# Output product of self-attention: one of eight stationary tiles dropped, its rows carried by transfers between buffers

## What is computed

```python
Wdkv = x @ latent_w + latent_b
q = jnp.einsum('btc,hcl->bhtl', x, Wd_w) + Wd_b[None, :, None, :]
scores = jnp.einsum('bhtl,bsl->bhts', q, Wdkv) / sqrt(d_head)     # causal mask
attn = jax.nn.softmax(scores, axis=-1)
y = jnp.einsum('bhts,bsl->bhtl', attn, Wdkv)
z = jnp.transpose(y, (0, 2, 1, 3)).reshape(b, t, h * Wdkv.shape[-1])
return z @ out_w + out_b
```

## Time and profile before

| | us |
|---|---|
| median of 3 runs | 3112.0 |
| lowest and highest of them | 3110.74, 3114.18 |
| the profiled execution's own time | 3109.21 |
| its span, first to last instruction | 3107.3 |
| mean granted clock of TensorE, share of full | 0.998 |

### The profile page before, as it was taken

How to read it: one execution, slowest core, us unless ns; L and a number is a source line. 1 busy time by engine, 2 the same in 40 slices (tenths; PEclk the granted TensorE clock), 3 DMA queues, 4 the chain that set the end, 5 groups by cost and what they waited for, 6 DMA issues and landing times. The chain is left out here.

```text
span 3107.3 us, 72903 instructions
## 1 busy us (share of the span) xinstructions
PE 3080.1 (99%) x22657; PEld 2894.1 (93%) x22657; DVE 2259.1 (73%) x6587; ACT 2146.8 (69%) x6949; POOL 1591.9 (51%) x2918
## 2 busy tenths in 40 slices
PE   9999999999999999999999999999999999999998
PEld 7999999999999998999999999999988888889998
DVE  7888888887777877778878777887865555444665
ACT  8888888888888887787887877887744444442222
POOL 5677677666676665333333333333456666652000
PEclk9999999999999999999999999999999999999999
DMA  5455555444444460211111211211255445433333
GB/s 166 125 148 159 150 151 153 138 121 125 123 113 114 126 212 30 65 45 49 62 45 49 62 49 45 63 48 48 102 133 113 101 102 115 115 54 89 125 125 101
DMA packets 202273, 315.29 MB, mean 101 GB/s; under 512 B 34752, under 2 KB 135744, under 8 KB 200928
## 3 DMA queue, kind: packets, MB, share of 16 engines
q1 hardware_dynamic: 177376, 277.82, 29.6%
q0 software_dynamic: 24576, 33.57, 6.3%
HBM read 125.20 MB, written 75.50 MB: 65 GB/s over the span
## 5 line engine op out<-in xcount | busy, mean ns | idle before, releaser
L1131 POOL TENSOR_SCALAR ca_prob<-ca_prob,ca_inverse 128x120 f32<-128x120 f32 x1024 | 354.7, 365 | 618.9 <-DVE ca_inverse L1433 616.9
L820 ACT ACTIVATE sa_prob<-sa_prob,sa_shift 128x128 f32<-128x128 f32 (+1 forms) x1024 | 453.7, 462 | 0.0
L1373 ACT ACTIVATE ca_prob<-bank,ca_shift 128x120 f32<-128x120 f32 x1024 | 354.9, 368 | 3.5 <-DVE ca_shift L1427 2.2
L875 DVE CUSTOM_DVE_ANT_0 sa_prob<-bank,sa_mask 128x128 f32<-128x128 f32 (+1 forms) x1024 | 304.3, 351 | 0.9 <-issue 0.2
L566 POOL TENSOR_SCALAR sa_prob<-sa_prob,sa_inverse 128x128 f32<-128x128 f32 x512 | 199.4, 389 | 199.0 <-DVE sa_inverse L887 190.2
L137 PE MATMUL bank<-sa_ow,sa_y_hi 128*128 128x256 f32 x1024 | 278.1, 303 | 0.0
L139 PE MATMUL bank<-sa_kvT_b,sa_q 112*128 112x128 f32 (+1 forms) x1024 | 260.6, 280 | 0.0
L916 DVE TENSOR_TENSOR sa_pT_lo<-bank,sa_pT_hi 128x384 fp32r<-128x384 f32 x512 | 257.9, 543 | 0.2 <-ACT sa_pT_hi L807 0.2
L139 PE MATMUL bank<-sa_ow,sa_y_lo 112*128 112x256 f32 x1024 | 257.6, 282 | 0.0
L137 PE MATMUL bank<-sa_kvT_a,sa_q 128*128 128x128 f32 (+1 forms) x1024 | 248.9, 279 | 1.0 <-DVE sa_shift L875 0.7
L568 POOL TENSOR_SCALAR sa_prob<-sa_prob,sa_inverse 128x256 f32<-128x256 f32 x512 | 245.2, 479 | 0.0
(11 more groups left out here) (274 smaller groups left out, 12039.2 us busy)
## 6 DMA issues: line engine op xcount, KB each, us to landing
sa_q<-sa_q_tile SPq DMA_DIRECT2D x125, 288.0 KB
sa_q<-sa_q_tile SPq DMA_DIRECT2D x157, 112.0 KB
mid_x2T<-ca_x2T SPq DMA_DIRECT2D x32, 512.0 KB, 3.0
ex_sx<-mid_x2T SPq DMA_DIRECT2D x32, 512.0 KB, 3.4
sa_q<-sa_q_tile SPq DMA_DIRECT2D x297, 32.0 KB
sa_xT_raw<-in_xT SPq DMA_DIRECT2D x32, 256.0 KB, 2.9
sa_q<-sa_q_tile SPq DMA_DIRECT2D x32, 256.0 KB
sa_x_res<-in_x SPq DMA_DIRECT2D x32, 256.0 KB, 3.0
```

The lines of the kernel that those rows point to most:

```text
L820: act.activation(prob[:, r, hh, cols], prob[:, r, hh, cols], ACT.Exp, bias=shift[:, r, n:n + 1], scale=-1.0, accum_out=total[:, r, n:n + 1 ...
L875: dve.tensor_tensor_reduce(out=prob[:, r, hh, cols], in0=SC[hh][:, t * T:t * T + (t + 1) * P], in1=mask[:].rearrange("p a s -> p (a s)")[: ...
L1131: ins = pool.tensor_scalar(prob[:, r, t, hh], prob[:, r, t, hh], inverse[:, r, n:n + 1], 1.0, ALU.mult, ALU.mult)
L1373: act.activation(prob[:, r, t, hh], SC[g % 2][:, n * S:n * S + S], ACT.Exp, bias=shift[:, r, n:n + 1], accum_out=total[:, r, n:n + 1]).the ...
```

## The change

Four heads (two pairs of one sequence, `QUAD` = 4 slots: g and g+1 hold the first pair of sequence 0 and 1, g+2 and g+3 the second) now use seven stationary tiles in place of eight. The low tile of the first head is dropped. Its 88 rows (72 low rows and 16 high rows) are put into the empty rows of the low tiles of the other three heads: 24 rows into the second head's (`y_near`), 24 + 16 into the third's and 24 into the fourth's (`y_far`). As SBUF rows sit on partitions, this is four DMAs on SP for each first-pair slot g, issued in slot g+10, behind that slot's query moves. The first waits for `ylo_done`, the others also for the output product of slot g-2, whose buffer they write. DVE now writes 72 rows instead of 96; POOL copies 16 rows of one head instead of two in first-pair slots. PE waits for `y_near` before the low tile of the second head (slot g+12) and for `y_far` in the second pair (slot g+14). The high tiles of both heads now come first. The weights are laid out to match, on the host side of the program, and `split_ow` works in two instructions.

```diff
@@ SP, in slot(J, m), behind the query moves @@
+            g = m - PL
+            if slot_exists(J, g) and g % QUAD < 2:
+                r, i = g % RING, g % 2
+                need_alone(sp, ylo_done, upto_slot(J, g), spare_sp)
+                sp.dma_start(f32(y_lo[L:AT, r, 1]), f32(y_lo[0:GAP, r, 0])).then_inc(y_near[i], 16)
+                n = (g + 2) % RING
+                need(sp, o_mm, upto_slot(J, g - 2))
+                sp.dma_start(f32(y_lo[L:AT, n, 0]), f32(y_lo[GAP:2 * GAP, r, 0])).then_inc(y_far[i], 16)
+                sp.dma_start(f32(y_lo[P - REST:P, n, 0]), f32(y_hi[0:REST, r, 0])).then_inc(y_far[i], 16)
+                sp.dma_start(f32(y_lo[L:AT, n, 1]), f32(y_lo[2 * GAP:L, r, 0])).then_inc(y_far[i], 16)
@@ POOL @@
-                pool.tensor_scalar(y_lo[AT:AT + REST, r], f32(y_hi[0:REST, r]), 1.0, 1.0, ALU.mult, ALU.mult).then_inc(ydup_done, 1)
+                own = slice(int(g % QUAD < 2), 2)
+                pool.tensor_scalar(y_lo[AT:AT + REST, r, own], f32(y_hi[0:REST, r, own]), 1.0, 1.0, ALU.mult, ALU.mult).then_inc(ydup_done, 1)
@@ PE @@
-                for hh in range(2):
+                ahead = (y_near if p % 2 == 0 else y_far)[i]
+                for a, hh in ((0, 0), (0, 1), (1, 1)) if p % 2 == 0 else ((0, 0), (0, 1), (1, 0), (1, 1)):
                     w = slice((2 * p + hh) * C, (2 * p + hh + 1) * C)
+                    if a == 1 and hh == 1 - p % 2:
+                        need(pe, ahead, upto_quad(J, g, 16 if p % 2 == 0 else 48))
+                    rows = slice(0, AT + REST if a == 1 and (p % 2 == 0 or hh == 1) else P)
                     for t in range(TT):
                         tk = slice(t * P, t * P + P)
-
-                        mm = two(pe, O[i][:, t * C:t * C + C], y_hi[:, r, hh, tk], y_lo[:, r, hh, tk], ow[:, 0, w],
-                                 ow[:, 1, w], p == 0 and hh == 0 and t == 0, p == NP - 1 and hh == 1)
+                        mm = pe.matmul(O[i][:, t * C:t * C + C], (y_lo if a else y_hi)[rows, r, hh, tk], ow[rows, a, w],
+                                       start=p == 0 and a == 0 and hh == 0 and t == 0, stop=p == NP - 1 and a == 1 and hh == 1,
+                                       skip_group_check=True)
                 mm.then_inc(o_mm, 1)
@@ ACT @@
+                if g % QUAD < 2:
+                    need(act, y_far[g % 2], upto_quad(J, g - QUAD, 48))
                 act.activation(y_hi[:, r].rearrange("l h t -> l (h t)"), PV[:], ACT.Copy).then_inc(yhi_done, 1)
@@ DVE @@
-            dve.scalar_tensor_tensor(out=part, in0=f32(part), scalar=minus_low[:, 0:1], in1=raw,
-                                     op0=ALU.mult, op1=ALU.add).then_inc(ow_done, 1)
+            for a in range(2):
+                cols = slice(C if a == 1 and p % 2 == 0 else 0, 2 * C)
+                dve.scalar_tensor_tensor(out=part[:, a, cols], in0=f32(part[:, a, cols]), scalar=minus_low[:, a:a + 1], in1=raw[:, a, cols],
+                                         op0=ALU.mult, op1=ALU.add).then_inc(ow_done, 1)
-                dve.tensor_tensor(y_lo[0:AT, r].rearrange("l h t -> l (h t)"), PV[0:AT, :],
-                                  f32(y_hi[0:AT, r].rearrange("l h t -> l (h t)")), ALU.subtract).then_inc(ylo_done, 1)
+                dve.tensor_tensor(y_lo[0:L, r].rearrange("l h t -> l (h t)"), PV[0:L, :],
+                                  f32(y_hi[0:L, r].rearrange("l h t -> l (h t)")), ALU.subtract).then_inc(ylo_done, 1)
```

More of the change, by code:

```diff
@@ L178 @@
 SA_BODY = 32
+QUAD = 4
+GAP = AT - L
 SA_BODIES = B * NP // SA_BODY
@@ L202, in upto_tile, with upto_quad @@
     return J * (SA_GROUPS * QT * per) + (per * (t + 1) + more)
+def upto_quad(J, g, per=1):
+    return J * (SA_BODY // QUAD * per) + per * (g // QUAD + 1)
 def slot_exists(J, g):
@@ L283, in self_attention @@
     qbias, lbias, hbias = al.sb("qbias", [P, QT]), al.sb("lbias", [P, 1]), al.sb("hbias", [P, DIRECT])
-    minus_low = al.sb("minus_low", [P, 1])
+    minus_low = al.sb("minus_low", [P, 2])
     mask = al.sb("mask", [P, 3, P])
@@ L343, in self_attention @@
     ydup_done = al.sem("ydup_done")
+    y_near, y_far = [al.sem(f"y_near{i}") for i in range(2)], [al.sem(f"y_far{i}") for i in range(2)]
     q_mm, qhi_done, qlo_done = al.sem("q_mm"), al.sem("qhi_done"), al.sem("qlo_done")
@@ L376, in self_attention @@
     STAGE_FROM, STAGE_STEP = 40, 6
-    sthi_done, stlo_done = Later(owhi_done, NP), Later(ow_done, NP)
+    sthi_done, stlo_done = Later(owhi_done, NP), Later(ow_done, 2 * NP)
     WV_IN, WK_IN, WQ_HI_IN, WQ_LO_IN, WO_IN = 0, 1, 2, 4, 6
@@ L518, in slot @@
                     if m == at:
-                        sp.wait_ge(ow_done, p - OW_RING + 1)
+                        sp.wait_ge(ow_done, 2 * (p - OW_RING + 1))
                         load_ow(p)
@@ L541, in gpsimd @@
         pool.affine_select(out=minus_low[:], in_=minus_low[:], compare_op=ALU.is_ge, fill=0.0, base=-L,
-                           pattern=[[0, 1]], channel_multiplier=1).then_inc(const, 1)
+                           pattern=[[-GAP, 2]], channel_multiplier=1).then_inc(const, 1)
         pool.affine_select(out=mask[:, 0], in_=mask[:, 0], compare_op=ALU.is_ge, fill=MASKED, base=0,
@@ L725, in slot @@
                 if first_body(J) and c == 0 and i == 0:
-                    pe.wait_ge(ow_done, p + 1)
+                    pe.wait_ge(ow_done, 2 * (p + 1))
                 if p == 0:
                     need(pe, o_read, upto_row(J, c, i - 2))
-                for hh in range(2):
+                ahead = (y_near if p % 2 == 0 else y_far)[i]
+                for a, hh in ((0, 0), (0, 1), (1, 1)) if p % 2 == 0 else ((0, 0), (0, 1), (1, 0), (1, 1)):
                     w = slice((2 * p + hh) * C, (2 * p + hh + 1) * C)
+                    if a == 1 and hh == 1 - p % 2:
+                        need(pe, ahead, upto_quad(J, g, 16 if p % 2 == 0 else 48))
+                    rows = slice(0, AT + REST if a == 1 and (p % 2 == 0 or hh == 1) else P)
                     for t in range(TT):
                         tk = slice(t * P, t * P + P)
-                        mm = two(pe, O[i][:, t * C:t * C + C], y_hi[:, r, hh, tk], y_lo[:, r, hh, tk], ow[:, 0, w],
-                                 ow[:, 1, w], p == 0 and hh == 0 and t == 0, p == NP - 1 and hh == 1)
+                        mm = pe.matmul(O[i][:, t * C:t * C + C], (y_lo if a else y_hi)[rows, r, hh, tk], ow[rows, a, w],
+                                       start=p == 0 and a == 0 and hh == 0 and t == 0, stop=p == NP - 1 and a == 1 and hh == 1,
+                                       skip_group_check=True)
                 mm.then_inc(o_mm, 1)
@@ L2324, with filled @@
     ow = a("L0_attn_out_w").reshape(H, L, C).transpose(1, 0, 2).reshape(L, H * C)
+    def filled(h):
+        own, lent, n = ow[:, h * C:(h + 1) * C], ow[:, (h - h % QUAD) * C:(h - h % QUAD + 1) * C], h % QUAD
+        rows = np.zeros((P, C), ow.dtype)
+        if n > 0:
+            rows[:L], rows[L:AT], rows[AT:AT + REST] = own, lent[(n - 1) * GAP:n * GAP], own[:REST]
+        if n == 2:
+            rows[AT + REST:] = lent[:REST]
+        return rows
     laid = {
@@ L2331 @@
         "ow_a": again(ow, 0),
-        "ow_b": np.concatenate((ow, np.zeros((AT - L, H * C), ow.dtype), ow[:REST], np.zeros((P - AT - REST, H * C), ow.dtype))),
+        "ow_b": np.concatenate([filled(h) for h in range(H)], 1),
         "qbias": a("L0_attn_Wd_b").reshape(QT, P).T, "lbias": again(a("L0_attn_latent_b").reshape(L, 1), 0),
```

## The result

| | before | after |
|---|---|---|
| median | 3111.7 us | 3280.4 us |
| lowest and highest | 3110.7, 3114.2 | 3276.4, 3286.3 |
| span of the profiled execution | 3107.3 | 3278.9 |
| mean granted clock in it | 0.998 | 0.975 |

The account below looks back on a forecast made before the run. PE was taken as the bound, with SP overbooked by the change: 3109.2 + 90 (stops) + 15 (weight issues) - 1 (last slots) + 12 (clock) = 3225 us, 3228 on the median's scale; range 3160 to 3285.

Parts of the forecast that it names:

- The bound and the sign: Self-attention: PE is the bound before; 32 more issues per group overbook SP (1047 us against PE's 973); slower, 0.88.
- The removed matmuls: First-pair slots of self-attention: two of eight output matmuls gone in 256 slots, 30.7 us less.
- The price of a small issue: SP, first-pair slots: 0.77 us per 24-row DMA, 0.61 for 16 rows, gap included; 2.9 us per slot.
- The landing of 2.0: `y_near` transfers of 24 KB in self-attention: taken to land 2.0 us after issue.
- The laying-out of the group: Self-attention group: PE stops 2.0, 2.4, 3.5 us in slots 5, 8, 13; 6.0 us longer, 90 over 15 groups.
- The clock term: Behind slot 13's stop the granted clock may fall: 0 to 1.7 us per group, 12 us taken in all.
- The weight issues: SP: 48 weight issues over some six groups, about 5 each ahead of slot 11's `y_near`; 15 us more.
- The end: Last slots of self-attention, behind the query moves, keep their gain: -1 us.
- The faster ones: SP's issues overlap or small moves are quick: 3081 us, 8%; break-even at 0.4 to 0.45 each: 3106 to 3118, 4%.
- The worse one: Clock falls at most stops and SP carries debt onward, or moves take their maxima: 3275 to 3330 us, 8%.
- its own case: Self-attention: SP overbooked, PE stops for `y_near`: 3228 us, low end 3166, high end 3271; 70%.

Follow-up runs that it names:

- e4: Kernel before, all its matmuls kept, plus 32 idle small issues per group on SP that nobody waits for: 3183.6 us, 1.0241.
- e2: Changed kernel without any small transfers, their waits, or the part of the output product that needs them: 3082.4 us, 0.991 of the kernel before.
- e7: Changed kernel with both sequences' far transfers paired on SP (12 small issues per group left) and `y_near` issued by ACT: 3098.9 us, 0.9962.
- e5: Changed kernel with both sequences' far transfers made as three DMAs instead of six, 20 small issues per group instead of 32: 3198.4 us, 1.0278.
- e12: Changed kernel with 12 extra output matmuls in slot 5 of every group, ahead of the wait for `y_near`: 3272.0 us, 1.0524.
- e3: Changed kernel with `y_near` alone, 8 small issues per group instead of 32, the `y_far` rows left out of the product: 3112.8 us, 1.0012.
- e8: e7 with the cross-attention weight transfers begun later and spread wider (8 slots apart from slot 45, not 6 from 40): 3094.4 us, 0.9949.
- e9: e8 with the second pair of 1 MB weight loads issued from slot 260 on instead of 258: 3095.5 us, 0.9956.
- e1: Changed kernel with `y_near` issued ahead of a slot's query moves instead of behind them: 3287.5 us, 1.0569.
- e11: Changed kernel with 20 extra output matmuls in slot 13 of every group, ahead of the wait for `y_near`: 3268.6 us, 1.0511.

## Why the prediction was right, and where its size was off

**The bound and the sign.** Right. The reading that SP, which is missing from the table of busy engines, had no room for 32 more issues is shown from four sides: the chain with 17% of SP, e4 with the issues alone, e2 without them, and e7 with a part of them on another engine.

**The rule of the Trainium skill.** Issues on SP held it for 0.55 to 0.83 us, and 32 more per group cost 5.5% of the kernel, or 2.4% where PE waits for none of them (e4). On this, "DMA: Bandwidth & Descriptors", section "Issuing engines are not separate DMA queues", calls the sequencer's time to initiate a DMA usually small relative to the DMA; here an issue of 0.73 us stands beside 1.98 us to use, and moving 8 of 20 small issues per group to another sequencer saved 100 us (e5 to e7). The measurement decides.

**The removed matmuls, 30.7 us.** Right: e2 shows 28 to 29.

**The price of a small issue.** Right: 2.92 us per slot measured for 2.9 taken, 24 rows at 0.73, 16 rows at 0.55 to 0.57. The landing of 2.0 was right too.

**The laying-out of the group.** `y_near` of slots 3, 6 and 11 was forecast at 18.1, 33.8 and 58.7 us behind the start of slot 2; in the group above it is issued at 18.7, 34.1 and 58.7. PE goes on at 20.6, 36.1 and 60.7 (forecast 20.1, 35.8, 60.7). The stops are 2.2, 0.3 and 3.0 for 2.0, 2.4 and 3.5. The one in slot 8 is short because the clock had fallen behind the first: PE arrived late by itself. The prediction says so ("a loss at the first two only shortens the next stop"), and e12, where the clock stays up behind slot 5, shows it: the stop in slot 8 is some 1.5 us or more in 13 of 14 cases, and the time is not told apart from the change's. Total of the stops: 110.9 us for some 118 by the laying-out (110 in the prediction's last paragraph).

**The clock term** is the first term that was mis-sized. It was bounded by one row, a loss of 1.7 us behind a stop of 2.18, and 0.8 per group was taken. Measured behind slot 13 is a mean of 1.8, with up to 3.4, twice what that row lost. A bound from a single stop was no upper bound. From slot 13's stop to the next slot 2 PE needed 20.2 us in the group shown and some 19.5 in the mean of the six later groups, for 17.4 (18.2 with the clock term) forecast. SP's `y_near` of slot 11 was 0.6 us later than forecast in their mean. A plain group is 8.8 us longer than before, for 6.8 forecast with the clock term: 30 us over 15 groups.

**The weight issues** are the second. 2.5 us for each of six groups were forecast; seven groups had 3.4 above the plain ones, 9 us more, and the first group, with the loads of `out_w`, 3 more, which had not been counted. Part of this is stops in a place that the laying-out had in time: of six in slot 0, 10.9 us in all, five fall into these eight groups. e3 and e4 missed upwards in the same groups.

**The end** is the third: -1 was forecast. But SP puts loads of 1 MB in front of the `y_near` of slot 258, for which PE stops in slot 260:

```profile
1309.69 0.95 SPq L460 DMA_DIRECT2D cross_wk_hi<-mid_cw  x1
1310.68 0.44 SPq L460 DMA_DIRECT2D cross_wk_lo<-mid_cw  x1
1311.16 0.44 SPq L460 DMA_DIRECT2D cross_wq_hi<-mid_cw  x1
1311.73 0.76 SPq L523 DMA_DIRECT2D sa_y_lo<-sa_y_lo  x1
...
1324.82 0.58 PE L756 MATMUL bank<-sa_ow,sa_y_lo 112*128 112x256 f32 x1 [7.38 <-DMA sa_y_lo<-sa_y_lo]
```

The issue ends at 1312.49 and PE goes on at 1324.82. A 24 KB transfer that is of use 2 us behind its issue elsewhere needed 13.1 us here. That the loads delay it, even where another engine issues it, is shown by e8 and e9, in which ACT issues one `y_near` at the same instant. In e8 these loads are issued ahead of it, and PE goes on 7.1 us behind its issue:

```profile
1127.07 0.44 SPq L460 DMA_DIRECT2D cross_wk_lo<-mid_cw  x1
1127.56 0.48 SPq L460 DMA_DIRECT2D cross_wq_hi<-mid_cw  x1
...
1131.94 0.73 ACTq L848 DMA_DIRECT2D sa_y_lo<-sa_y_lo  x1
...
1139.07 0.50 PE L753 MATMUL bank<-sa_ow,sa_y_lo 112*128 112x256 f32 x2 [0.94 <-DMA sa_y_lo<-sa_y_lo]
```

In e9 these loads come behind it, and PE does not stop there:

```profile
1131.93 0.73 ACTq L848 DMA_DIRECT2D sa_y_lo<-sa_y_lo  x1
...
1134.69 0.73 SPq L460 DMA_DIRECT2D cross_wk_hi<-mid_cw  x1
...
1137.95 0.40 PE L753 MATMUL bank<-sa_ow,sa_y_lo 112*128 112x256 f32 x2
```

By the trace's semaphore events the transfer landed 7.1 us behind its issue in e8 and 2.1 in e9. The later small transfers of e9 then wait behind the moved loads, with stops of 1.5, 0.9 and 2.4 us for e8's 0.9, 2.0 and 0.8. In the change, the part behind the last mark is 20.1 us longer, 11.3 more than a plain group explains, for -1 forecast. So the profiled executions are 171.6 us apart where 116 were forecast, and the 55.6 that are missing are 29.6 of the plain groups, 9.1 of the weight issues, 3.4 of the first group, 12.3 of the end and 1.2 of the start. (The medians are 169 apart.)

**The rivals.** The faster ones fell with the price of the issues. The worse one (3275 to 3330: the clock falls at most stops, and debts) came half true: the clock did fall behind 11 of 15 stops in slot 13, but SP carried no debt into the next group; it stood still for 4.8 to 7.5 us before the first query move of the six later groups. The measured time lies at that case's lower edge, 9 us above the high end (3271) that the prediction gave its own case, and 5 below the top of the range. The range holds it because it was stretched to take in the edge of this rival; the case's own terms were too small by some 55 us together.

## What to carry to other kernels

Before work is put on the engine that issues transfers, add up its issues in its own timeline, at the price by row count, and lay them out against the due times; the table of busy engines doesn't show that load. If it is full, order alone does not help (e1), nor do fewer bytes per row (24 rows hold SP 0.73 us at 2 KB per row, L514, and at 1 KB, L523); fewer issues or another issuer do (here ACT, with room for 0.74 us in every first-pair slot). Price a stop of PE with the clock behind it, from several stops rather than one, and only where no later wait swallows the loss.

## What the runs showed of the hardware

- **The clock behind a short stop.** In the change, e11 and e12 there are 124 stops for `y_near` in slots 5, 8 and 13. Behind the 38 below 1.4 us the granted clock of the next 8 us was 1.00 each time. Of the 21 from 1.4 to 1.8 it fell behind 9, of the 32 from 1.8 to 2.5 behind 22, of the 33 longer ones behind 30. Mostly it was 0.79 over these 8 us, in 15 cases below 0.75. Why the same length goes either way is left open here.
- **Work instead of a stop can be faster.** 20 extra matmuls per group saved some 11 us (1.0511 [1.0494, 1.0529] against 1.0545 [1.0532, 1.0557]).
- **Two pieces per row cost issue time**: 0.79 to 0.83 us for 24 rows and 0.68 for 16, against 0.73 and 0.55 for one piece. Such a DMA moves twice the bytes, and so 1.6 to 1.9 times as much per us of SP.
- **A small transfer behind 1 MB loads** took 13.1 us to use instead of 2.0 in the change; issued from ACT it landed after 7.1 us behind them (e8) and after 2.1 ahead of them (e9).
